# A two-layer graph block on one core: layer-one gates from row sums on VectorE, basis products in fours, and the layer norm's powers between the root weight's lower parts

## The chip, the cores and the metric

One core of a Trainium2 chip runs the whole program. The metric is device time in microseconds (us) for one execution. Five engines work side by side, each through its own queue of instructions: TensorE (PE in the profile, its weight loads PEld), VectorE (DVE), ScalarE (ACT), GpSimd (POOL) and SyncE (SP), which here issues the large loads. They hand work to each other with semaphores. The time that counts is the median of several executions; the profile shows one more, with its own time.

## The reference

625 nodes with 512 features, 20,625 edges of two types. First a graph convolution with batch norm, exact GELU and two residual sums, then a layer norm; its result is `x1`. On `x1` run two gated relational layers, and their sum with `x1` is normalised again:

```python
def rgcn_gate_layer(x, row, col, edge_type, basis, att, gate_w, root, bias):
    w = jnp.einsum('rb,bio->rio', att, basis)        # 30 bases of 512x512 -> 2 weights
    x_j = x[col]
    for r in range(NUM_RELATIONS):
        gate = jax.nn.sigmoid(x_j @ gate_w[r, :, 0])
        msgs.append(gate[:, None] * x_j @ w[r])
    msg = jnp.where((edge_type == 0)[:, None], msgs[0], msgs[1])
    agg = jax.ops.segment_sum(msg, row, num_segments=x.shape[0])
    return agg + x @ root + bias
...
h = relu(rgcn_gate_layer(x1, ..., basis1, ...)); out = rgcn_gate_layer(h, ..., basis2, ...)
```

A gate depends only on the node and the relation, so the kernel computes 625 x 2 gates and 625 x 2 products `Z` per layer and multiplies with count matrices of the edges afterwards.

## The kernel before

Nodes go in 5 chunks of 125 rows (`NC`), features in 4 blocks of 128 (`KC`). Matrix products of layers one and two run in single precision from two parts, an upper part rounded to fp32r and a lower part with the rest: `mm3` issues upper x upper, upper x lower and lower x upper (L542 to L544).

**The basis.** 64 parts of 1 MB (`basis_part`, L561) are contracted with the attention weights on TensorE: parts 0 to 31 for layer one, 32 to 63 for layer two. They go through a ring of 4 slots, `basis_ring`. SyncE issues the load of part n when part n - 4 has been used. `basis_upto(n)` places parts in TensorE's stream between other work, up to part n. 4 parts make one PSUM tile of `psW` (two tiles, used in turn), 8 parts one of 8 pairs of weight blocks. ScalarE empties the first tile (`w_first`), VectorE merges the second (`w_merge`), ScalarE makes the upper part (`w_high`) and VectorE the lower part (`w_low`).

**From the convolution to `x1`.** The convolved rows pass GELU on ScalarE, feature block by feature block, and are turned back on TensorE (L733). VectorE adds the residual (`x_sum`) and takes each chunk's mean and variance. GpSimd raises the variance to the power -0.5 (L518) and makes the bias (L519). ScalarE normalises (L962, `xs`), TensorE turns each chunk (`x1_turned`, L749), ScalarE and VectorE make the upper and lower parts in `hlT` (`x1_hi` L954, `x1_lo` L1281). The root weight is split by ScalarE (`root_hi`, L950) and GpSimd (`root1_low`, L511). GpSimd's stream puts three of the four lower parts ahead of the first power.

**Layer one.** 8 root products (2 halves of the nodes x 4 feature blocks) follow, with chunks 3 and 4 turned between them. Then `gates_and_z`: gate products of both halves (L779, 16 records), the first `Z`, the sums of their pairs (L799, 10 records), then the other nine `Z` of 12 matmuls each; TensorE waits for all of the layer's lower weight parts first. ScalarE copies the gate rows, takes the sigmoid and scales `Z` into `zg` (L998, L1328). Then 8 products `h` with the count matrices (L816), whose results become the next `hlT` (L1354, L1013, L1358).

**Layer two** is `gates_and_z(1)` again, then 5 chunks of `out` (root products and L836), the last layer norm and the stores. Four PSUM tiles of `psM` pass through a fixed list of uses; TensorE takes a tile when the use four places earlier has been emptied.

The order on every engine is written out by hand.

## Time and profile before

| | |
|---|---|
| median of 3 runs | 302.01 us (300.69 to 302.09) |
| the profiled execution | 302.61 us, its span 300.8 us |
| TensorE busy | 272.3 us, 91% of the span |
| VectorE / ScalarE / GpSimd busy | 158.6 / 84.4 / 48.0 us |
| mean granted TensorE clock | 0.983 of full |
| HBM read | 72.05 MB |

The span is the stretch between the first and the last recorded event of one execution; the remaining 1.8 us lie around it. Busy time says how long an engine worked, not whether the end of the program waited for it; the chain of waits says that. In timelines a row is: start, duration, engine, line, operation, output and inputs, shapes, number of instructions merged into the row, and in brackets the idle time before it with what ended it. The ends of matmuls are modelled, so the distance between two starts is the better measure.

### The profile page before, as it was taken

How to read it: one execution, taken by the hardware profiler on the slowest of the kernel's cores; microseconds unless marked ns; L12 is line 12 of the kernel's file. 1: busy time of each engine (PE TensorE's matmuls, PEld its weight loads, DVE VectorE, ACT ScalarE, POOL GpSimd, SP SyncE). 2: the span in 40 equal slices, each digit the busy share in tenths (PEclk: the TensorE clock that was granted, in tenths of full speed). 3: DMA queues.
4: the chain of work that ended last, by engine and by line, in shares of the span. 5: the costliest groups of instructions: out<-in, count | busy, mean ns of one | idle time of the engine just before them, and what ended most of it. 6: DMA issues, size and time to landing. Idle time of an engine off the chain costs nothing.

```text
span 300.8 us, 4592 instructions
## 1 busy us (share of the span) xinstructions
PE 272.3 (91%) x1687; PEld 182.4 (61%) x1687; DVE 158.6 (53%) x340; ACT 84.4 (28%) x143; POOL 48.0 (16%) x90
## 2 busy tenths in 40 slices
PE   0899889999799975999999999999989999999991
PEld 0784334335477742647666465677777787778770
DVE  6788878888738868726301412434242234234443
ACT  3351021003437586261531140114113242000000
POOL 5531000000681019000000000000009100011111
PEclk9999999999979999799999999999999999999997
DMA  6999999999899998999949788775004200001112
GB/s 170 222 418 385 403 403 405 407 380 349 300 287 340 367 386 331 392 377 391 382 168 419 279 358 340 278 264 237 2 0 105 72 1 0 0 2 34 34 34 68
DMA packets 12803, 73.64 MB, mean 245 GB/s; under 512 B 2000, under 2 KB 2243, under 8 KB 4588
## 3 DMA queue, kind: packets, MB, share of 16 engines
q1 hardware_dynamic: 11330, 70.82, 62.4%
q0 software_dynamic: 1104, 2.36, 3.1%
q8 instruction: 13, 0.21, 0.3%
q10 hardware_dynamic: 346, 0.17, 0.2%
q14 instruction: 10, 0.08, 0.1%
HBM read 72.05 MB, written 1.28 MB: 244 GB/s over the span
## 4 chain that ended last, share of the span: by engine, by line
PE 65%; DVE 14%; issue 6%; DMA 5%; ACT 4%; POOL 3%; DVEq 2%; SPq 0%; POOLq 0%; ACTq 0%
PE psW L561 12%; PE psM L542 9%; PE psM L543 8%; PE psM L544 8%; PE psM L816 8%; PE psM L836 6%; PE psM L692 3%; DVE B L1130 3%; DMA xs<-in_x_dram 3%; DMA basis_ring<-in_L_gnn_basis_dram 3%; PE psE L649 2%; POOL root_lo L511 2%; DVE w_full L1107 1%; PE psM L602 1%; DVEq L1120 1%
## 5 line engine op out<-in xcount | busy, mean ns | idle before, releaser
L561 PE MATMUL psW<-basis_ring,S 128*32 128x512 f32 x512 | 63.0, 608 | 2.4 <-DMA basis_ring<-in_L_gnn_basis_dram 2.0
L1328 DVE SCALAR_TENSOR_TENSOR zg<-psM,gate,zg 125x512 fp32r<-125x512 f32 x20 | 15.0, 750 | 57.0 <-ACT zg L998 57.0
L542 PE MATMUL psM<-w,hlT 128*125 128x512 f32 x80 | 32.4, 406 | 0.1
L561 PEld LDWEIGHTS psW<-basis_ring,S 128*32 128x32 f32 x512 | 13.3, 110 | 30.4 <-issue 21.1
L544 PE MATMUL psM<-w,hlT 128*125 128x512 f32 x80 | 31.6, 395 | 0.0
L543 PE MATMUL psM<-w,hlT 128*125 128x512 f32 x80 | 31.6, 395 | 0.0
L998 ACT ACTIVATE zg<-psM,gate 125x512 fp32r<-125x512 f32 x20 | 13.8, 689 | 46.3 <-PE psM L544 45.9
L649 PEld LDWEIGHTS psE<-oh_key,oh_src 128*125 128x125 f16 x162 | 14.0, 143 | 19.3 <-issue 15.6
L816 PEld LDWEIGHTS psM<-BB,zg 125*128 125x128 f32 x160 | 23.1, 188 | 3.4 <-issue 2.5
L816 PE MATMUL psM<-BB,zg 125*128 125x320 f32 (+1 forms) x160 | 24.1, 309 | 0.0
L836 PE MATMUL psM<-zg,BB 125*125 125x512 f32 x100 | 24.0, 394 | 0.0
L526 POOL DMA_DIRECT2D root_raw<-in_L_gnn_root_dram x16 | 7.9, 502 | 97.0 <-DVE hlT L1358 97.0
L1130 DVE TENSOR_TENSOR B<-B,psE 125x160 f32 x54 | 17.4, 323 | 8.5 <-issue 3.4
L836 PEld LDWEIGHTS psM<-zg,BB 125*125 125x125 f32 x100 | 18.6, 186 | 4.7
L616 PE MATMUL psM<-w0T,xT 128*125 128x512 f32 x40 | 20.3, 609 | 0.0
L542 PEld LDWEIGHTS psM<-w,hlT 128*125 128x125 f32 x80 | 14.8, 185 | 9.0 <-issue 2.5
L649 PE MATMUL psE<-oh_key,oh_src 128*125 128x160 f16 x162 | 17.2, 245 | 3.4 <-DVE B L1130 3.1
L1137 DVE TENSOR_TENSOR oh_key<-iota_f,key_pairs 128x960 f16<-128x960 f16 x27 | 18.1, 670 | 0.2
L544 PEld LDWEIGHTS psM<-w,hlT 128*125 128x125 f32 x80 | 14.8, 185 | 3.8
L543 PEld LDWEIGHTS psM<-w,hlT 128*125 128x125 f32 x80 | 14.8, 185 | 3.4
L692 PE MATMUL psM<-AT,z 125*128 125x320 f32 (+1 forms) x80 | 15.1, 340 | 1.6 <-DVE z L1223 1.6
L692 PEld LDWEIGHTS psM<-AT,z 125*128 125x128 f32 x80 | 13.0, 209 | 4.5 <-issue 3.5
(153 smaller groups left out, 385.0 us busy)
## 6 DMA issues: line engine op xcount, KB each, us to landing
basis_ring<-in_L_gnn_basis_dram SPq DMA_DIRECT2D x64, 1024.0 KB, 7.4
root_raw<-in_L_gnn_root_dram POOLq DMA_DIRECT2D x32, 64.0 KB, 2.9
xs<-in_x_dram SPq DMA_DIRECT2D x1, 1120.0 KB
out_dram<-xs SPq DMA_DIRECT2D x5, 224.0 KB
w_raw<-in_L_gnn_W_dram SPq DMA_DIRECT2D x4, 256.0 KB, 9.1
bias_b<-in_L_gnn_bias_dram POOLq DMA_DIRECT2D x1, 250.0 KB, 3.9
xs<-in_x_dram SPq DMA_DIRECT2D x1, 130.0 KB
out_dram<-xs SPq DMA_DIRECT2D x5, 26.0 KB
```

The source lines that it names most:

```text
L542: nc.tensor.matmul(o, l_hi, r_hi, start=start, stop=False)
L543: nc.tensor.matmul(o, l_hi, r_lo, start=False, stop=False)
L544: last[0] = nc.tensor.matmul(o, l_lo, r_hi, start=False, stop=stop)
L561: m = nc.tensor.matmul(psW[32 * j:32 * j + 32, cc % 2, :], S[:, cc % 2, cc // CH, q].rearrange("p k r -> p (k r)"), ring[:, n % RING, j, : ...
L616: last[0] = nc.tensor.matmul(bank(("xw", c))[0:PC, :], xT[:, k, n], w0T[:, k], start=(k == 0), stop=(k == KC - 1))
L649: nc.tensor.matmul(psE[0:PC, g % 2, at:at + KEYS], oh_src[:, g % 3, j * P:j * P + PC], oh_key[:, t % OH, :], start=(j % SG == 0), stop=(j ...
L692: last[0] = nc.tensor.matmul(bank(("agg0", f, h))[:, 0:n], z[:, i, s, f * P:(f + 1) * P], AT[:, s, a:a + n], start=(s == 0 and i == 0), st ...
L816: last[0] = nc.tensor.matmul(bank(("h", f, h))[:, 0:n], zg[:, i, d, r, f * P:(f + 1) * P], BB[:, at:at + n], start=(d + r + i == 0), stop= ...
L836: last[0] = nc.tensor.matmul(bank(("out", c))[0:PC, :], BB[:, at:at + PC], zg[:, i, d, r, :], start=False, stop=(d == NC - 1 and r + i == 2))
L1130: v.tensor_tensor(to, to, psE[0:PC, g % 2, h * KEYS:(h + 1) * KEYS] .rearrange("p (c t w) -> p c t w", c=NC, t=R), ALU.add).then_inc(win_a ...
L1137: return v.tensor_tensor(out, pair.unsqueeze(1).broadcast_to(shape), pairs[:, first:first + n].unsqueeze(2).broadcast_to(shape), ALU.is_equal)
L1328: link(v.scalar_tensor_tensor(out=zg[:, 1, c, r, :], in0=bank(("Z", L, c, r))[0:PC, :], scalar=gate[:, L, c, r:r + 1], in1=zg[:, 0, c, r, ...
```

## The change

- VectorE computes layer one's gates: GpSimd loads each gate vector of layer one into all 125 partitions (`gate_raw`, two DMAs ahead of the root weight's sixteen), ScalarE reorders them (`gate_q`, two copies before the third GELU), and VectorE takes ten row sums of `xs` times gate (`gates_dotted`), eight of them ahead of chunk 3's lower part. ScalarE's sigmoid reads these sums. TensorE has no gate work in layer one.
- In layer two each half's gate rows come just before the first `Z` that needs them, and the pair sums come in two groups.
- A `Z` waits for each lower weight part where it uses it.
- `basis_upto` is called with numbers that place four parts at a time from part 36 on.
- `w_merge(7)`, `w_high(7)` and `w_low(7)` stand earlier among the `h` products' results.
- GpSimd alternates: one lower part of the root weight, the power and bias of a chunk.

```diff
+            for r in range(R):
+                pool.dma_start(gate_raw[0:PC, r, :], gate1[r:r + 1, :, 0].broadcast_to([PC, D])).then_inc(gate1_in, 16)
...
-            for k in range(KC - 1):
-                root1_low(k)
             for c in range(NC):
+                if c < EARLY - 1:
+                    root1_low(c)
                 pool.wait_ge(var_ready, KC + 1 + c)
                 link(nc.gpsimd.tensor_tensor(lrs[:, c:c + 1], lrs[:, c:c + 1], mhalf[0:PC, 0:1], ALU.pow))
...
                 if c == EARLY - 1:
-                    root1_low(KC - 1)
+                    for k in range(c, KC):
+                        root1_low(k)
...
-                    basis_upto((35, 37, 39, 39, 41, 41, 43, 43)[KC * h + f])
+                    basis_upto((35, 39, 39, 39, 39, 43, 43, 43)[KC * h + f])
...
-                pe.wait_ge(w_lo, R * KC * (L + 1))
...
+                            pe.wait_ge(w_lo, R * (KC * L + k) + r + 1)
...
-                            basis_upto((45, 47, 47, 49, 51, 51, 53, 55, 55, 57)[R * c + r])
+                            basis_upto((43, 47, 47, 51, 51, 51, 55, 55, 55, 59)[R * c + r])
...
-                    basis_upto((57, 59, 59, 61, 61, 63, 63, 63)[KC * h + f])
-            gates_and_z(1)
+                    basis_upto((59, 59, 63, 63, 63, 63, 63, 63)[KC * h + f])
+            z_products(1)
...
+                if f == KC - 1:
+                    act.wait_ge(gate1_in, 16 * R)
+                    for r in range(R):
+                        nc.scalar.activation(in_q(gate_q[0:PC, r]), natural(gate_raw[0:PC, r]), ACT.Copy) \
+                            .then_inc(gate_q_ready, 1)
...
+                if L == 0:
+                    act.wait_ge(gate_dots, R * NC)
+                    link(nc.scalar.activation(gate[:, 0], gate_dot[:], ACT.Sigmoid))
...
-            w_high(7)
-            gates_and_z(1)
+                    if i == 5:
+                        w_high(7)
...
+            def gates_dotted(c):
+                dve.wait_ge(x1_ready, c + 1)
+                for r in range(R):
+                    link(v.scalar_tensor_tensor(out=gate_raw[0:PC, r], in0=xs[:, c, :], scalar=1.0, in1=gate_q[0:PC, r],
+                                                op0=ALU.mult, op1=ALU.mult, accum_out=gate_dot[:, c, r:r + 1]))
+                    dve.sem_inc(gate_dots, 1)
...
+            dve.wait_ge(gate_q_ready, R)
+            for c in range(NC - 1):
+                gates_dotted(c)
             x1_lo(3)
             w_low(2)
             x1_lo(4)
+            gates_dotted(NC - 1)
...
+                    if i == 4:
+                        w_merge(7)
                     if i == 6:
-                        w_merge(7)
-            w_low(7)
+                        w_low(7)
```

GpSimd, from the root weight's lower parts (`root_lo`) to chunk 3's power (`lrs`) and bias (`lnm`), before:

```order
L511 TENSOR_TENSOR root_lo<-root_raw,root_hi 128x512 x3
L518 TENSOR_TENSOR lrs<-lrs,mhalf 125x1
L519 TENSOR_TENSOR lnm<-lnm,lrs 125x1
L518 TENSOR_TENSOR lrs<-lrs,mhalf 125x1
L519 TENSOR_TENSOR lnm<-lnm,lrs 125x1
L518 TENSOR_TENSOR lrs<-lrs,mhalf 125x1
L519 TENSOR_TENSOR lnm<-lnm,lrs 125x1
L511 TENSOR_TENSOR root_lo<-root_raw,root_hi 128x512
```

And the same place now:

```order
L519 TENSOR_TENSOR root_lo<-root_raw,root_hi 128x512
L526 TENSOR_TENSOR lrs<-lrs,mhalf 125x1
L527 TENSOR_TENSOR lnm<-lnm,lrs 125x1
L519 TENSOR_TENSOR root_lo<-root_raw,root_hi 128x512
L526 TENSOR_TENSOR lrs<-lrs,mhalf 125x1
L527 TENSOR_TENSOR lnm<-lnm,lrs 125x1
L526 TENSOR_TENSOR lrs<-lrs,mhalf 125x1
L527 TENSOR_TENSOR lnm<-lnm,lrs 125x1
L519 TENSOR_TENSOR root_lo<-root_raw,root_hi 128x512 x2
```

The first power stands behind one lower part instead of three; the first three chunks' powers are past two lower parts, and two lower parts come behind them.

VectorE, from chunk 4's statistics of `x_sum` to the gate vectors' parts for layer two (`gw_hl`), before:

```order
L1289 BN_STATS lst<-x_sum 125x6
L1295 BN_AGGR lag<-lst 125x2
L1296 TENSOR_SCALAR lnm<-lag 125x1
L1265 TENSOR_SCALAR lrs<-lag 125x1
L1281 TENSOR_TENSOR hlT<-psM,hlT 128x4x125
L1116 TENSOR_TENSOR w<-w_full,w 128x512 x2
L1281 TENSOR_TENSOR hlT<-psM,hlT 128x4x125
L1316 CAST gw_hl<-vecT 128x8x2
```

Now:

```order
L1325 BN_STATS lst<-x_sum 125x6
L1331 BN_AGGR lag<-lst 125x2
L1332 TENSOR_SCALAR lnm<-lag 125x1
L1301 TENSOR_SCALAR lrs<-lag 125x1
L1339 SCALAR_TENSOR_TENSOR gate_raw,gate_dot<-xs,gate_q 125x512 x8
L1317 TENSOR_TENSOR hlT<-psM,hlT 128x4x125
L1152 TENSOR_TENSOR w<-w_full,w 128x512 x2
L1317 TENSOR_TENSOR hlT<-psM,hlT 128x4x125
L1339 SCALAR_TENSOR_TENSOR gate_raw,gate_dot<-xs,gate_q 125x512 x2
L1364 CAST gw_hl<-vecT 128x8x2
```

Eight row sums stand ahead of chunk 3's lower part (`hlT`), two behind chunk 4's.

TensorE, the last basis parts of layer two and the start of layer two's products, before (`BB,zg` are the `h` products, `hlT,gw_hl` the gate rows, `w,hlT` the first `Z`):

```order
L816 MATMUL psM<-BB,zg 128x320 x40
L561 MATMUL psW<-basis_ring,S 32x512 x8
L816 MATMUL psM<-BB,zg 128x306 x40
L561 MATMUL psW<-basis_ring,S 32x512 x8
L816 MATMUL psM<-BB,zg 128x306 x40
L779 MATMUL psM<-hlT,gw_hl 4x320 x8
L779 MATMUL psM<-hlT,gw_hl 4x306 x8
L542 MATMUL psM<-w,hlT 125x512
```

Now:

```order
L830 MATMUL psM<-BB,zg 128x320 x60
L570 MATMUL psW<-basis_ring,S 32x512 x16
L830 MATMUL psM<-BB,zg 128x320 x20
L830 MATMUL psM<-BB,zg 128x306 x80
L786 MATMUL psM<-hlT,gw_hl 4x320 x8
L551 MATMUL psM<-w,hlT 125x512
```

Three pairs of parts among the `h` products have become one four, and only the first half's gate rows stand ahead of the first `Z`. The rows count matmuls as written; the profile has two records for each of `psW`, the gate rows and the pair sums.

## Rows read from the trace of the kernel before

**Rows 1.** The page: the chain that ended last, by engine.
```profile
PE 65%; DVE 14%; issue 6%; DMA 5%; ACT 4%; POOL 3%; DVEq 2%; SPq 0%; POOLq 0%; ACTq 0%
```
**Rows 2.** Timeline before layer two: TensorE alone, start and duration first.
```profile
222.84 1.32 PE L779 MATMUL psM<-hlT,gw_hl 128*4 128x320 f32 x8
225.88 1.28 PE L779 MATMUL psM<-hlT,gw_hl 128*4 128x306 f32 x8 [1.71 <-DVE hlT L1358]
227.21 0.50 PE L542 MATMUL psM<-w,hlT 128*125 128x512 f32 x1
```
**Rows 3.** Timeline before layer one's `Z`: gate rows, first `Z`, pair sums.
```profile
147.87 2.44 PE L779 MATMUL psM<-hlT,gw_hl 128*4 128x320 f32 x16
150.15 0.39 PE L542 MATMUL psM<-w,hlT 128*125 128x512 f32 x1
153.02 1.25 PE L799 MATMUL psM<-pair_sum,gate_rows 4*125 4x2 f32 x10
```
**Rows 4.** Timeline of TensorE, one pair of basis parts among the root products.
```profile
138.53 0.30 PE L544 MATMUL psM<-hlT,root_lo 128*128 128x306 f32 x1
138.76 1.92 PE L561 MATMUL psW<-basis_ring,S 128*32 128x512 f32 x16
140.62 0.41 PE L542 MATMUL psM<-hlT,root_hi 128*128 128x306 f32 x1
144.21 1.07 PE L561 MATMUL psW<-basis_ring,S 128*32 128x512 f32 x8
```
**Rows 5.** Timeline from the fourth GELU to the normalised chunks, several engines.
```profile
108.76 0.91 ACT L944 ACTIVATE hf<-hf,bn 128x625 f32<-128x625 f32 x1 [0.78 <-DVE bn L1234]
110.71 4.03 ACT L950 ACTIVATE root_hi<-root_raw 128x512 fp32r<-128x512 f32 x4
111.85 4.59 POOL L511 TENSOR_TENSOR root_lo<-root_raw,root_hi 128x512 fp32r<-128x512 f32 x3 [3.79 <-ACT root_hi L950]
116.36 0.58 POOL L518 TENSOR_TENSOR lrs<-lrs,mhalf 125x1 f32<-125x1 f32 x1
117.31 1.53 ACT L962 ACTIVATE xs<-x_sum,lnm,lrs 125x512 f32<-125x512 f32 x2 [2.57 <-POOL lnm L519]
```
**Rows 6.** Timeline of the basis parts 30 to 35 on TensorE.
```profile
111.95 2.78 PE L561 MATMUL psW<-basis_ring,S 128*32 128x512 f32 x24
115.92 1.07 PE L561 MATMUL psW<-basis_ring,S 128*32 128x512 f32 x8 [1.19 <-DMA basis_ring<-in_L_gnn_basis_dram]
121.23 2.99 PE L561 MATMUL psW<-basis_ring,S 128*32 128x512 f32 x16
122.69 0.45 PEld L561 LDWEIGHTS psW<-basis_ring,S 128*32 128x32 f32 x8 [1.26 <-DMA basis_ring<-in_L_gnn_basis_dram]
```
**Rows 7.** Stretches: busy us by engine, granted clock, DMA share, GB/s.
```profile
113.10:114.20 1.10, 1.10 (x16) 0.28 (x8) 1.06 (x5) 1.10 (x2) 1.10 (x2) 1.00 0.41 82
114.20:152.20 38.00, 34.41 (x237) 21.84 (x230) 19.67 (x45) 17.37 (x30) 7.29 (x13) 0.96 0.98 384
152.20:156.10 3.90, 3.90 (x31) 2.00 (x29) 0.60 (x1) 0.89 (x3) 0.00 (x0) 1.00 0.07 29
156.10:166.80 10.70, 10.70 (x59) 7.03 (x60) 1.65 (x3) 1.42 (x3) 0.00 (x0) 1.00 0.99 390
```
**Rows 8.** The ring's tile: its loads from issue to landing.
```profile
DMA to landing us min/median/max: 4.7/7.4/18.5
```
**Rows 9.** VectorE: chunk 3's lower part, and a linked operation with two inputs.
```profile
133.49 0.68 DVE L1281 TENSOR_TENSOR hlT<-psM,hlT 128x500 fp32r<-128x500 f32 x1 [5.29 <-ACT hlT L954]
138.71 0.74 DVE L1102 SCALAR_TENSOR_TENSOR w_half<-psW,mask_h,w_half 128x512 f32<-128x512 f32 x1
110.13 1.02 DVE L1274 SCALAR_TENSOR_TENSOR x_sum<-xs,psM 125x512 f32<-125x512 f32 x1 [1.41 <-PE psM L733]
```
**Rows 10.** Stretches ahead of the spell of low clock and in it; the page's clock.
```profile
116.00:120.50 4.50, 2.58 (x18) 1.21 (x19) 3.33 (x8) 3.17 (x5) 4.00 (x8) 0.95 1.01 415
120.50:123.80 3.30, 3.30 (x20) 0.96 (x18) 2.23 (x4) 0.72 (x2) 0.00 (x0) 0.56 1.00 420
PEclk9999999999979999799999999999999999999997
```

More of the change, by code:

```diff
@@ L182, in gnn_block @@
         gate = sb("gate", [PC, 2, NC, R], F32)
+        gate_dot = sb("gate_dot", [PC, NC, R], F32)
         psM = ctx.enter_context(nc.psum_tensor("psM", [P, 4, 512], F32))
@@ L285, in gnn_block @@
                     use(("x1T", LATE[h, f]), "dve")
+        ROWS_AT = {(0, 0): 0, (1, 0): 1}
+        GATE_AT = {(0, 0): 0, (1, 0): 1}
+        GATED = (range(0, HALF[0][1] // PC), range(HALF[0][1] // PC, NC))
         for L in range(2):
-            for h in range(2):
-                use(("gate_rows", L, h), "act")
             for c in range(NC):
                 for r in range(R):
+                    if L == 1 and (c, r) in ROWS_AT:
+                        use(("gate_rows", ROWS_AT[c, r]), "act")
                     use(("Z", L, c, r), "dve")
-                    if (c, r) == (0, 0):
-                        use(("gate", L), "act")
+                    if L == 1 and (c, r) in GATE_AT:
+                        use(("gate", GATE_AT[c, r]), "act")
             if L == 0:
@@ L766, in _, with gate_rows_of, gates_turned, z_products @@
                         x1_turned(LATE[h, f])
[L767 to L784 removed]
+                    basis_upto((35, 39, 39, 39, 39, 43, 43, 43)[KC * h + f])
+            def gate_rows_of(h):
+                a, n = HALF[h]
+                pe.wait_ge(gw_ready, 1)
+                pe.wait_ge(t_ready, NC + (h + 1) * KC)
+                wait_free(pe, ("gate_rows", h))
+                for k in range(KC):
+                    for i in range(2):
+                        last[0] = nc.tensor.matmul(bank(("gate_rows", h))[0:2 * R, 0:n],
+                                                   gw_hl[:, 1, k].rearrange("p i r -> p (i r)"),
+                                                   hlT[:, i, k, a:a + n], start=(k + i == 0),
+                                                   stop=(k == KC - 1 and i == 1))
+                done()
+            def gates_turned(h):
+                pe.wait_ge(gate_rows_ready, h + 1)
+                wait_free(pe, ("gate", h))
+                for i, d in enumerate(GATED[h]):
+                    last[0] = nc.tensor.matmul(bank(("gate", h))[0:PC, R * i:R * i + R],
+                                               gate_rows[:, d * PC:(d + 1) * PC], pair_sum[:], start=True, stop=True)
+                done()
+            def z_products(L):
                 for c in range(NC):
@@ L793, in gates_and_z @@
                         done()
-                        if (c, r) == (0, 0):
-                            pe.wait_ge(gate_rows_ready, 2 * (L + 1))
-                            wait_free(pe, ("gate", L))
-                            for d in range(NC):
-                                last[0] = nc.tensor.matmul(bank(("gate", L))[0:PC, R * d:R * d + R],
-                                                           gate_rows[:, d * PC:(d + 1) * PC], pair_sum[:],
-                                                           start=True, stop=True)
-                            done()
+                        if L == 1 and (c, r) in GATE_AT:
+                            gates_turned(GATE_AT[c, r])
                         if L == 0:
-                            basis_upto((45, 47, 47, 49, 51, 51, 53, 55, 55, 57)[R * c + r])
-            gates_and_z(0)
+                            basis_upto((43, 47, 47, 51, 51, 51, 55, 55, 55, 59)[R * c + r])
+            z_products(0)
             for h, (a, n) in enumerate(HALF):
@@ L999, in gates_and_z @@
                                              scale=gate[:, L, c, r:r + 1]).then_inc(zg_hi, 1)
+                        if L == 1 and (c, r) == (1, 0):
+                            gates_of(1)
                     if L == 0 and c == 2:
@@ L1322, in z_parts @@
             def z_parts(L):
-                dve.wait_ge(gate_ready, L + 1)
                 for c in range(NC):
+                    dve.wait_ge(gate_ready, L + 1 + (L == 1 and c in GATED[1]))
                     for r in range(R):
```

57 lines of the change are left out of this document (27 added, 30 removed).

## The prediction

> **What bounds the kernel now.** I read the chain of waits first: TensorE carries 65% of what ended last, and no other engine more than 14% [rows 1]. So work taken off TensorE counts in full, unless TensorE then waits for something else. The timelines of its gaps come next. Before layer two it stands still for 1.71 us until the last block of `hlT` is ready [rows 2]. Before layer one it waits twice for basis parts, part 33 until 115.92 and part 35 until 122.69 [rows 6]. Last come the stretches by DMA share: from 114.2 to 152.2 the DMA engines are 98% busy, with no reserve, and only later do they pause, at a share of 0.07 from 152.2 to 156.1 [rows 7]. The reader should keep two regimes apart: until about 150 the ring of basis parts sets the pace together with TensorE, afterwards TensorE alone does.
>
> **What TensorE loses.** Layer one's gate rows: from 147.87 to the first `Z` at 150.15 are 2.3 us, less one normal step, 2.1 us [rows 3]. Layer one's pair sums: 1.25 us, 1.2 after the same step [rows 3].
>
> The fours: one more part within a group costs 2.78 - 1.92 = 0.86 us [rows 4, 6]. A pair costs more than 2 x 0.86 = 1.72: from the last root matmul's start ahead of it at 138.53 to the first one's behind it at 140.62 are 2.09 us, less one normal step of 0.14, so 1.95 [rows 4]; the two root products behind it take 3.59 us up to 144.21, some 0.05 of that a slow first step. That makes a seam of about 0.28. Fourteen pairs (36 to 63) become seven fours: 7 x 0.28 = 2.0 us. A four takes 3.7.
>
> Layer two's seam: the wait of 1.71 us goes, since the first half's gate rows and the first two chunks' `Z` need nothing of the second half, and block 7's weight parts, now made two `h` products earlier, no longer end at 227.2. What is late next is the sigmoid of two chunks; it has a whole `Z` of 2.9 us [rows 3] ahead of it, and four PSUM tiles. Two more seams take back what is left of the gap up to 227.21. I take 1.7.
>
> Together 7.0 us, if nothing starves.
>
> **The front, with the GpSimd move.** The power of chunk 0 stands behind 4.59 us of lower parts, 1.53 each, and ScalarE idles 2.57 us for it [rows 5]. Behind one part it would be 3.06 us earlier. But ScalarE gets two reordering copies ahead of the third GELU. They have no row; the nearest is `root_hi` with the same reordering, 4.03 / 4 = 1.0 us each [rows 5]. The fourth GELU, at 108.76, had 0.78 us of idle time before it [rows 5], which hides that much. Bounds: 0 if the copies ran in idle time altogether, 2.0 if nothing hid them; I take 2.0 - 0.8 = 1.2 us. Everything behind moves by that: `root_hi` 110.7 to 111.9, its end 114.7 to 115.9. ScalarE can normalise chunk 0 only then, at about 116.0 instead of 117.31. A power with its bias takes about 0.8 (from 116.36 to shortly before 117.31). Chunk 2's ended at 116.36 + 2.4 = 118.8 before; now it comes behind two lower parts and two powers, 113.05 + 3.06 + 2.4 = 118.5. The last lower part ends 1.4 us later, near 121.7, and the root products cannot start before 35 in any case. So the two edits nearly cancel there.
>
> Part 35 decides. It landed at 122.69, and SyncE could issue it only when part 31 had been used, 1.7 us into the group at 111.95 [rows 6]. That group stands behind GELU and moves with it, up to 1.2 us. The DMA engines had nothing but stragglers at that moment (share 0.41 in 113.1 to 114.2 [rows 7]), so the load may land up to 1.2 later, or at the same time if the straggler sets it. I take +0.35 us for the root products' start, bounds -0.5 and +1.2.
>
> The two loads of gate vectors add 0.5 MB, 1.3 us of the rate of 390 GB/s, at 82 us, and two issues ahead of sixteen on GpSimd's queue; the root weight is not read before 110.7, so nothing waits. Bounds 0 and 1.3, taken 0.
>
> **VectorE's row sums.** No row shows this form. The nearest linked operation takes 0.74 us, a reordered one 1.02 [rows 9]. VectorE was idle for 5.29 us ahead of chunk 3's lower part at 133.49, so it was free from 128.2 [rows 9]. With 0.8 each, eight sums end at 128.2 + 6.4 = 134.6, 1.1 us later than that start. Chunk 4's part then ends at about 138.4, and the fifth root product, which needs it, comes at about 138.8. That costs nothing; with 1.02 each the product would wait 1.5 us.
>
> **What starves.** The ring has four slots. A load alone takes 4.7 us to land [rows 8]; four loads in a row take 10.7 us of the DMA engines [rows 7], 2.67 each. So the fourth lands 1.0 + 4.7 + 3 x 2.67 = 13.7 us after a four begins, and is wanted 2.75 us into the next. Two fours must be 11 us apart. At the first one (36 to 39) parts 38 and 39 are issued only when 34 and 35 have been used, before at about 122 and at 124.2 [rows 6]. Behind 35 at 122.69 four loads of 2.67 give 133.4; with the front's delay 134.1. TensorE wants it at 124.2 + 0.35 + two products (3.6) + chunk 3's turn (an estimate of 0.6: four small transposes) + three parts (2.6) = 131.4. It waits 2.7 us; bounds 1.5 and 4. Between the second and third four lie more than 11 us, fine. The fourth (48 to 51) follows after two `Z` only, 3.7 + 5.6 = 9.3 us: it waits 1.4; bounds 0.6 and 3. The others are 12 us apart or more: 0.
>
> **Sum.** 302.61 - 7.0 + 0.35 + 2.7 + 1.4 = 300.06. I round the waits down by 0.1, to 299.9, since chunk 2's power comes 0.3 us earlier. The profiled execution lies 0.6 above the median of the runs, so I forecast 299.3 us as a median, 0.9% less. About 0.5% (1.5 us) is what can be told from no change.
>
> **Rivals.**
>
> A: the ring does not starve, because the stragglers and not the issues set the landing. For it: in all pairs behind 150 TensorE never waited for a part. Against it: a DMA share of 0.98 up to 152. Then 302.0 - 7.0 + 0.35 = 295.4.
>
> B, slower: the new waits cost TensorE its clock. Before, 4.5 us with 2.58 busy were followed by 3.3 us at a granted clock of 0.56, near the lower of its two levels, 1.2 GHz [rows 10]; work of 3.3 x 0.44 = 1.45 us was lost. If each of three places (in front of the root products longer than now, at the first four, at the fourth) brought one such spell, 4.35 us would be added: 299.3 + 4.35 = 303.7. It decides from the second spell on: two give 302.2. Against it: the wait of 1.71 us before layer two [rows 2] brought no spell, the clock's digits there are all 9 [rows 10]. The Trainium skill says on this, in "TensorE: Matmul & The Clock Gate", section "The HAM clock gate", that the throttled state is the default and activity releases it, so a starved TensorE is slowed again; by that rule the longer wait at the first four would be followed by slow products, by the row of 1.71 us it would not.
>
> C: the change does not do what it says at the front and VectorE is late. Row sums at 1.02 to 1.1 us hold the fifth root product back by 1.5 to 2, and part 35 lands the full 1.2 late: 299.3 + 1.5 + 0.85 = 301.6, no measurable change.
>
> **How the numbers follow.** Forecast 0.48, its own range 297.8 to 300.8; A 0.20; B 0.17; C 0.15. Eight in ten: from A's 295.2 up to 302.6, where half of B is left out. Faster by over 0.5% (below 300.5): 0.46 of the forecast, 0.20 of A, 0.04 of C, 0.70. Same: 0.02 + 0.10 of C + 0.04 of B = 0.16. Slower: 0.14.
>
> **What would show it.** Right: the root products start near 124.5; TensorE waits for `basis_ring` by 2 to 3 us in the first four and by about 1.4 in the one after the fourth `Z`; layer one's first `Z` starts within half a microsecond of 150.15; the last `h` product ends near 222.5; the first `Z` of layer two follows 1.3 us behind. ScalarE normalises chunk 0 near 116.0, after `root_hi`, not after a power. Wrong: no waits for the ring at the fours (A), a granted clock near 0.5 behind one (B), or a fifth root product that VectorE releases (C). If `xs` for chunk 0 started near 114 the reordering copies cost nothing, and the front would gain too.

## The result, and the profile after

| | before | after |
|---|---|---|
| median | 302.05 us (4 runs, 300.69 to 303.11) | 298.75 us (4 runs, 296.8 to 301.16) |
| the profiled execution, its span | 302.61, 300.8 us | 299.43, 297.6 us |
| TensorE busy | 272.3 us | 267.4 us |
| VectorE busy | 158.6 us | 165.3 us |

The ratio is 0.9899 with an interval of 0.9861 to 0.9936, so the kernel became 1.0% faster; 299.3 was forecast. Beside three other kernels on another chip the same kernel had 298.63 us and 0.9896 [0.9852, 0.994]. The total is right, but it is a sum of terms of which one, the start of the root products, was far off, and others made up for it. The chain that ended last, by engine:

```profile
PE 63%; DMA 19%; DVE 8%; issue 4%; ACT 2%; DVEq 2%; POOL 1%; SPq 0%; POOLq 0%; ACTq 0%
```

TensorE kept its share, and DMA went from 5% [rows 1] to 19%. Waits for the ring replace the work taken off TensorE. The timeline of TensorE after the change, at the waits and at the start of each stage:

```profile
98.40 1.06 PE L570 MATMUL psW<-basis_ring,S 128*32 128x512 f32 x8
101.92 1.06 PE L570 MATMUL psW<-basis_ring,S 128*32 128x512 f32 x8 [2.46 <-DMA basis_ring<-in_L_gnn_basis_dram]
113.96 5.34 PE L570 MATMUL psW<-basis_ring,S 128*32 128x512 f32 x32
122.34 1.06 PE L570 MATMUL psW<-basis_ring,S 128*32 128x512 f32 x8 [0.44 <-DMA basis_ring<-in_L_gnn_basis_dram]
124.83 1.07 PE L570 MATMUL psW<-basis_ring,S 128*32 128x512 f32 x8 [1.43 <-DMA basis_ring<-in_L_gnn_basis_dram]
125.83 0.41 PE L551 MATMUL psM<-hlT,root_hi 128*128 128x320 f32 x1
132.28 1.06 PE L570 MATMUL psW<-basis_ring,S 128*32 128x512 f32 x8 [0.34 <-DMA basis_ring<-in_L_gnn_basis_dram]
143.09 0.30 PE L553 MATMUL psM<-hlT,root_lo 128*128 128x306 f32 x1
143.33 3.64 PE L570 MATMUL psW<-basis_ring,S 128*32 128x512 f32 x32
146.90 0.41 PE L551 MATMUL psM<-hlT,root_hi 128*128 128x306 f32 x1
147.15 0.30 PE L552 MATMUL psM<-hlT,root_hi 128*128 128x306 f32 x1
150.39 0.39 PE L551 MATMUL psM<-w,hlT 128*125 128x512 f32 x1
169.50 1.06 PE L570 MATMUL psW<-basis_ring,S 128*32 128x512 f32 x8 [1.31 <-DMA basis_ring<-in_L_gnn_basis_dram]
221.75 1.33 PE L786 MATMUL psM<-hlT,gw_hl 128*4 128x320 f32 x8
222.92 0.40 PE L551 MATMUL psM<-w,hlT 128*125 128x512 f32 x1
225.80 0.59 PE L797 MATMUL psM<-pair_sum,gate_rows 4*125 4x2 f32 x4
229.20 1.25 PE L786 MATMUL psM<-hlT,gw_hl 128*4 128x306 f32 x8
```

Part 27 now waits at 101.92, where before nothing waited (its group stands at 99.84 there, one row of 1.92 us). Part 35 starts at 124.83 instead of 122.69 [rows 6]. The root products start 1.7 us later than before (125.83 and 124.15), and layer one's first `Z` still comes at 150.39, against 150.15 [rows 3]. Layer two's first `Z` comes 1.17 us behind the first gate rows, where it was 4.37 us [rows 2]. ScalarE at the front, after:

```profile
107.02 2.02 ACT L957 ACTIVATE gate_q<-gate_raw 125x512 f32<-125x512 f32 x2
108.95 0.89 ACT L963 ACTIVATE hf<-hf,bn 128x625 f32<-128x625 f32 x1
110.79 0.89 ACT L963 ACTIVATE hf<-hf,bn 128x625 f32<-128x625 f32 x1
112.73 3.96 ACT L969 ACTIVATE root_hi<-root_raw 128x512 fp32r<-128x512 f32 x4
116.57 0.82 ACT L981 ACTIVATE xs<-x_sum,lnm,lrs 125x512 f32<-125x512 f32 x1
```

The copies take 1.01 us each. The fourth GELU comes at 110.79 against 108.76 [rows 5], and chunk 0 is normalised at 116.57 right behind `root_hi`; its power and bias end at about the same time, at 116.42.

### The profile page after: what moved, and what is told of

It reads as the page before. It is cut to its first block, busy times and chain, and to the rows that moved or that the text cites. A ratio compares the mean times of both kernels' runs of the same rounds, so it can differ in the third digit from the quotient of the medians.

```text
span 297.6 us, 4596 instructions
## 1 busy us (share of the span) xinstructions
PE 267.4 (90%) x1661; PEld 179.6 (60%) x1661; DVE 165.3 (56%) x360; ACT 85.8 (29%) x144; POOL 49.6 (17%) x92
## 4 chain that ended last, share of the span: by engine, by line
PE 63%; DMA 19%; DVE 8%; issue 4%; ACT 2%; DVEq 2%; POOL 1%; SPq 0%; POOLq 0%; ACTq 0%
DMA basis_ring<-in_L_gnn_basis_dram 16%; PE psW L570 13%; PE psM L551 8%; PE psM L553 8%; PE psM L552 8%; PE psM L830 8%; PE psM L850 6%; PE psE L658 3%; DMA xs<-in_x_dram 3%; DVE B L1166 2%; PE psM L701 2%; PE psM L625 2%; PE psM L611 1%; DVEq L1156 1%; DVE oh_key L1173 1%
## 5 line engine op out<-in xcount | busy, mean ns | idle before, releaser
L570 PE MATMUL psW<-basis_ring,S 128*32 128x512 f32 x512 | 64.2, 624 | 8.2 <-DMA basis_ring<-in_L_gnn_basis_dram 7.9
L570 PEld LDWEIGHTS psW<-basis_ring,S 128*32 128x32 f32 x512 | 14.0, 112 | 41.2 <-issue 22.7
L1423 DVE TENSOR_TENSOR res<-res,psM 125x512 f32<-125x512 f32 x5 | 3.4, 688 | 21.2 <-PE psM L850 21.2
L1173 DVE TENSOR_TENSOR oh_src<-iota_f,place_pairs 128x756 f16<-128x756 f16 x27 | 14.9, 552 | 0.4 <-DVE w_full L1143 0.2
```

Source lines behind the costliest of these rows:

```text
L570: m = nc.tensor.matmul(psW[32 * j:32 * j + 32, cc % 2, :], S[:, cc % 2, cc // CH, q].rearrange("p k r -> p (k r)"), ring[:, n % RING, j, : ...
L1173: return v.tensor_tensor(out, pair.unsqueeze(1).broadcast_to(shape), pairs[:, first:first + n].unsqueeze(2).broadcast_to(shape), ALU.is_equal)
```

## The experiments

All edits are on the kernel after, except the two said to be on the kernel before. "Part 27" gives the wait in front of that part and "root" the start of the root products, both in the profiled execution, in us; "-" means that this profile isn't used.

| | median, runs | ratio to before [95%] | part 27 | root |
|---|---|---|---|---|
| after | 298.75, 4 | 0.9899 [0.9861, 0.9936] | 2.46 | 125.83 |
| after, on a second chip | 298.63, 6 | 0.9896 [0.9852, 0.994] | 2.04 | 126.24 |
| GpSimd's order of before | 299.77, 12 | 0.9945 [0.991, 0.9979] | 2.17 | 127.89 |
| basis parts in pairs | 298.62, 6 | 0.9898 [0.9866, 0.9931] | 2.75 | 125.86 |
| copies late | 297.95, 6 | 0.9884 [0.9856, 0.9911] | 0 | 123.01 |
| copies late, second chip | 297.04, 6 | 0.9858 [0.9808, 0.9909] | 0 | 122.68 |
| copies late, pairs | 298.54, 6 | 0.9879 [0.9839, 0.9918] | 2.63 | 124.71 |
| no gate loads | 298.59, 6 | 0.9886 [0.9853, 0.9919] | 0 | 125.10 |
| gate loads twice | 300.62, 12 | 0.9934 [0.9902, 0.9966] | - | - |
| block 7 late | 299.96, 12 | 0.9923 [0.9899, 0.9948] | 2.80 | 126.75 |
| pairs and fours mixed | 300.32, 9 | 0.992 [0.9886, 0.9955] | 0 | 125.02 |
| before with GpSimd's new order | 301.4, 12 | 0.996 [0.9935, 0.9985] | 0 | 122.45 |
| before with fours | 302.14, 12 | 0.9999 [0.9967, 1.0031] | 0 | 124.30 |

**GpSimd's order of before.** The edit on the kernel after:

```diff
+            for k in range(KC - 1):
+                root1_low(k)
             for c in range(NC):
-                if c < EARLY - 1:
-                    root1_low(c)
...
                 if c == EARLY - 1:
-                    for k in range(c, KC):
-                        root1_low(k)
+                    root1_low(KC - 1)
```

> The changed kernel with GpSimd's old order: three lower parts of the root weight ahead of the first power. Theory (basis parts set the start of the root products): chunk 0 is normalised about 2.7 us later (near 119.3 instead of 116.6), but part 35 still lands near 124.8, so the root products start at most 0.7 us later and the median is 298.7 to 299.5. Rival (the powers were on the path): the root products start 2 us or more later and the median rises to about 301.

The median rose by 1.0 us. In the profile the three lower parts (115.59, 4.57 us) stand ahead of the first power again and chunk 0 is normalised at 121.03; no part of the ring is waited for at 34 and 35, so the normalisation is the bound there. The root products come 2.06 us later than after, as the rival had it, though the median stays near the theory's range. The fairer profile beside it is the second one of the kernel after: it has the same spell of low clock behind part 27 and reaches part 30 at the same time (115.57, here 115.68), and its root products start at 126.24. Of the 1.65 us between the two, 0.1 stands there already, 1.1 is low clock over parts 34 and 35, and about 0.4 is the order itself:

```profile
124.95 3.01 PE L569 MATMUL psW<-basis_ring,S 128*32 128x512 f32 x16
```

From here to the first root product are 2.94 us; the same stretch at full clock, with no wait, takes 1.85 (late copies with pairs, 122.86 to 124.71). The kernel before has 2.92 (121.23 to 124.15 [rows 6]) and the kernel before with fours 2.96. So the clock was low over parts 34 and 35 in all three profiles with GpSimd's old order, where TensorE stood 2.4 to 2.6 us, in one wait or two, ahead of chunk 0's turn, and in none of the other ten compared. That the longer stand brings the low clock is argued from this, not shown.

**The kernel before with GpSimd's new order alone.** The same lines, the other way round:

```diff
-            for k in range(KC - 1):
-                root1_low(k)
...
+                if c < EARLY - 1:
+                    root1_low(c)
...
-                    root1_low(KC - 1)
+                    for k in range(c, KC):
+                        root1_low(k)
```

> The kernel before with GpSimd's new order alone. Theory (part 35 sets the start of the root products where GELU is not delayed): chunk 0 is normalised 2 us earlier, near 115, but part 35 still lands near 122.7 and the root products start at most 0.5 us earlier than 124.15; median 301.3 to 301.7. Rival (the powers were the path, as the changed kernel with the old order let one think, 1.1 us slower): the root products start 1.1 us or more earlier, median 300.6 or less.

0.4% faster (0.15 to 0.65). Chunk 0 is normalised at 114.49 instead of 117.31. TensorE:

```profile
119.26 1.07 PE L562 MATMUL psW<-basis_ring,S 128*32 128x512 f32 x8
121.46 1.06 PE L562 MATMUL psW<-basis_ring,S 128*32 128x512 f32 x8 [1.13 <-DMA basis_ring<-in_L_gnn_basis_dram]
122.45 0.41 PE L543 MATMUL psM<-hlT,root_hi 128*128 128x320 f32 x1
```

The root products start 1.70 us earlier than before, where the theory allowed 0.5 at most: the rival is right on the start, though the median lies in the theory's range. Part 34 comes 1.97 us earlier (121.23 before), and only now does TensorE wait for part 35. So in the kernel before the powers, and not part 35, held the root products back. Part of the 1.70 us is lost again at chunk 4's turn, which waits 1.01 us instead of 0.48.

**Basis parts in pairs**, the three lists of `basis_upto` as before:

```diff
-                    basis_upto((35, 39, 39, 39, 39, 43, 43, 43)[KC * h + f])
+                    basis_upto((35, 37, 39, 39, 41, 41, 43, 43)[KC * h + f])
...
-                            basis_upto((43, 47, 47, 51, 51, 51, 55, 55, 55, 59)[R * c + r])
+                            basis_upto((45, 47, 47, 49, 51, 51, 53, 55, 55, 57)[R * c + r])
...
-                    basis_upto((59, 59, 63, 63, 63, 63, 63, 63)[KC * h + f])
+                    basis_upto((57, 59, 59, 61, 61, 63, 63, 63)[KC * h + f])
```

> The changed kernel with basis parts placed in pairs as before (35, 37, 39, ... 63). Theory: seven more seams of 0.28 us cost 2.0 us, the waits of the fours for the ring (1.9 us at parts 38 and 39, 1.3 us at part 51) go, so the time is 1.2 us lower, 297.5. Rival (fours gain what their seams say): 2 us higher, 300.8.

No difference: 298.62 against 298.75, so neither expectation came true. The waits for the ring behind the root products' start go (3.03 us in the kernel after), and others come, of 0.4 and 0.75 us. TensorE in pairs, the rows that wait between 126 and 222 us:

```profile
134.31 0.41 PE L758 MATMUL psM<-ident,xs 125*128 125x125 f32 x2 [0.40 <-ACT r1T L993]
139.49 0.41 PE L551 MATMUL psM<-hlT,root_hi 128*128 128x306 f32 x1 [0.75 <-DVEq L1321]
```

The first row is chunk 4's turn, which waits for ScalarE. The kernel before has the same wait (132.70, 0.48 us), and the prediction had overlooked it. The second is the fifth root product: behind pairs it comes early enough to wait for VectorE, which is late by the row sums. In the kernel after the wait for the ring covers both.

**The kernel before with fours alone**, these three lists the other way round:

> The kernel before with nothing but the basis parts in fours. By the prediction's terms alone: -2.0 for seven seams, +2.7 and +1.4 for the waits at parts 36 to 39 and 48 to 51, so about +2.1, less what is absorbed later: 302.5 to 304. If the fours are worth what they cost, as they were on the changed kernel, it stays within 0.5 us of before, near 301.8. In the profile the waits should stand at the first and at the fourth group of four only.

Ratio 0.9999. TensorE there:

```profile
132.77 1.07 PE L561 MATMUL psW<-basis_ring,S 128*32 128x512 f32 x8 [1.37 <-DMA basis_ring<-in_L_gnn_basis_dram]
144.92 1.06 PE L561 MATMUL psW<-basis_ring,S 128*32 128x512 f32 x8 [0.77 <-DMA basis_ring<-in_L_gnn_basis_dram]
172.31 1.06 PE L561 MATMUL psW<-basis_ring,S 128*32 128x512 f32 x8 [1.39 <-DMA basis_ring<-in_L_gnn_basis_dram]
```

The waits stand at the first and the fourth four, as expected, and also at the second (144.92). Taken from start to start, the three fours last 4.3 us longer than undisturbed ones (their first parts are at 128.49, 141.37 and 168.14, and an undisturbed last part comes 2.58 us behind its first). Chunk 4's turn saves 0.7, the root products start 0.15 later, and the span grew by 1.6 (302.4 against 300.8), so the seven seams gave 4.3 + 0.15 - 0.7 - 1.6 = 2.1 us, 0.3 each. In the medians nothing is left of the 1.6. Both kernels say the same: fours exchange seams for waits.

**Pairs and fours mixed**, so that no four comes early:

```diff
-                    basis_upto((35, 39, 39, 39, 39, 43, 43, 43)[KC * h + f])
+                    basis_upto((35, 37, 39, 39, 39, 43, 43, 43)[KC * h + f])
...
-                            basis_upto((43, 47, 47, 51, 51, 51, 55, 55, 55, 59)[R * c + r])
+                            basis_upto((43, 47, 47, 47, 51, 51, 51, 55, 55, 57)[R * c + r])
```

> The changed kernel with basis parts placed for the ring: pairs for 36 to 39 and 56 to 59, fours elsewhere, and 48 to 51 one Z later, 52 to 55 one Z later. Theory (fours gain only where the ring is full): of the waits of 1.9 us at the first four about 0.4 are left, that of 1.3 us at part 51 goes, two more seams cost 0.6 us: 2.2 us lower, 296.5. Rival (the waits are only shifted to the next part, since the DMA rate sets them): same median as the changed kernel, 298.7.

It isn't better: the waits at parts 38 and 39 are gone, and the next four waits instead. TensorE, and one stretch (busy us by engine, granted clock, DMA share, GB/s):

```profile
144.23 1.06 PE L570 MATMUL psW<-basis_ring,S 128*32 128x512 f32 x8 [0.80 <-DMA basis_ring<-in_L_gnn_basis_dram]
146.71 1.93 PE L570 MATMUL psW<-basis_ring,S 128*32 128x512 f32 x8 [1.42 <-DMA basis_ring<-in_L_gnn_basis_dram]
```
```profile
146.00:151.00 5.00, 4.29 (x20) 2.62 (x21) 0.00 (x0) 1.27 (x2) 0.00 (x0) 0.66 1.02 423
```

The waits are 2.2 us here and 0.5 at 208.42, against 1.7 and 1.3 in the kernel after: about as much in either form, so they go with the rate of the loads more than with the grouping. And right behind this wait the clock is at 0.66 of full over 5 us, which loses another 5 x 0.34 = 1.7. That is rival B's mechanism.

**The copies late.** ScalarE copies the gate vectors only behind chunk 2's upper part (in the loop over the chunks, once `x1_hi(2)` is issued):

```diff
-                if f == KC - 1:
-                    act.wait_ge(gate1_in, 16 * R)
-                    for r in range(R):
-                        nc.scalar.activation(in_q(gate_q[0:PC, r]), ...
...
+                    act.wait_ge(gate1_in, 16 * R)
+                    for r in range(R):
+                        nc.scalar.activation(in_q(gate_q[0:PC, r]), ...
```

> The changed kernel with ScalarE's two reordering copies of the gate vectors moved from ahead of the third GELU into its idle time behind chunk 2's upper part. Theory (the copies delay GELU, with it the group of parts 30 to 33 and so the issue of part 35): the group starts 1.5 to 2 us earlier, part 35 lands 1 to 2 us earlier, the root products start about 1.5 us earlier, median 297.2. Rival (the DMA engines' rate sets part 35): it lands when it did, and the median stays at 298.7.

And once more beside the kernel after on one chip. The edit is the same two copies; the text below describes them wrongly (three copies, ahead of `root_hi`):

> The changed kernel with ScalarE's three copies of the gate rows behind the second chunk's normalisation instead of ahead of the root weight's upper parts. If the copies delay the front on the way to the root products (theory: they push x and the root weight's upper parts 2 us back, and about half of it reaches TensorE), the time is 0.7 to 1.0 us below the unaltered changed kernel beside it, near 298.0. If the front is set by the ring's transfers (rival: the third group of basis parts waits for its transfer whatever ScalarE does), it stays within 0.3 us of it.

Both are below the kernel after, by 0.8 and 1.6 us in the medians. With all runs of the two kernels, each divided by the median of before in its own comparison, the means have a ratio of 0.996 [0.992, 1.000] (12 and 10 runs): about 0.4%, at the edge of what can be told from nothing. Of the second, ScalarE and TensorE:

```profile
108.92 0.91 ACT L958 ACTIVATE hf<-hf,bn 128x625 f32<-128x625 f32 x1 [0.78 <-DVE bn L1269]
110.87 3.97 ACT L964 ACTIVATE root_hi<-root_raw 128x512 fp32r<-128x512 f32 x4
114.72 0.83 ACT L976 ACTIVATE xs<-x_sum,lnm,lrs 125x512 f32<-125x512 f32 x1
120.11 2.04 ACT L984 ACTIVATE gate_q<-gate_raw 125x512 f32<-125x512 f32 x2
```
```profile
100.00 1.93 PE L570 MATMUL psW<-basis_ring,S 128*32 128x512 f32 x16
112.11 3.64 PE L570 MATMUL psW<-basis_ring,S 128*32 128x512 f32 x32
121.68 1.06 PE L570 MATMUL psW<-basis_ring,S 128*32 128x512 f32 x8 [1.10 <-DMA basis_ring<-in_L_gnn_basis_dram]
122.68 0.42 PE L551 MATMUL psM<-hlT,root_hi 128*128 128x320 f32 x1
131.59 1.07 PE L570 MATMUL psW<-basis_ring,S 128*32 128x512 f32 x8 [1.39 <-DMA basis_ring<-in_L_gnn_basis_dram]
137.33 0.41 PE L551 MATMUL psM<-hlT,root_hi 128*128 128x306 f32 x1 [0.48 <-DVEq L1320]
```

GELU, `root_hi` and the group of parts 30 to 33 are back at their old places (112.11, before 111.95 [rows 6]), chunk 0 is normalised at 114.72, the copies lie in idle time, and the root products start 3.15 us earlier than after. That is more than the copies: in this execution part 27 isn't waited for, and no low clock lies on parts 30 to 33 (four parts in 3.64 us, after in 5.34). The sum is worked out below. The four parts behind keep their distance to part 35 (131.59 - 121.68 = 9.91; after 134.72 - 124.83 = 9.89), so the waits there don't grow with an earlier front.

**The copies late, with pairs**, the two edits above together.

> The same kernel with late copies, and the basis parts in pairs as in the kernel before. If fours only exchange seams (seven of about 0.28 us) for waits on the ring (about 1.8 to 2.7 us), pairs are the same to 0.5 us, 297.5 to 298.5. If the earlier front made the fours' waits longer (TensorE reaches parts 36 to 39 earlier than their transfers), pairs win here by about 1 us, 297.0.

298.54, 0.9879 [0.9839, 0.9918]: not told apart from the fours beside it. Chunk 4's turn waits 2.03 us for ScalarE, which is itself held up by chunk 4's power; the fifth root product doesn't wait. The clock is low behind this wait:

```profile
135.00:139.00 4.00, 4.00 (x21) 0.98 (x20) 3.32 (x9) 1.43 (x4) 0.00 (x0) 0.57 0.93 320
```

In this profile the next bound among the root products is the path of chunk 4, not the ring.

**Without the loads of the gate vectors.** The copies read rows of `x` instead, so layer one's gates come from other numbers; all work but the two loads is unchanged.

```diff
-            for r in range(R):
-                pool.dma_start(gate_raw[0:PC, r, :], gate1[r:r + 1, :, 0].broadcast_to([PC, D])).then_inc(gate1_in, 16)
...
-                        nc.scalar.activation(in_q(gate_q[0:PC, r]), natural(gate_raw[0:PC, r]), ACT.Copy) \
+                        nc.scalar.activation(in_q(gate_q[0:PC, r]), natural(xs[:, r, :]), ACT.Copy) \
```

> The changed kernel without the two loads of gate vectors; the reordering copies read rows of x instead, so layer one's gates are of other numbers. Theory (0.5 MB more on full DMA engines delay the basis parts): TensorE's wait of 2.46 us for part 27 near 99.5 falls to about 1.2 us or less and all behind it comes 1.2 us earlier, median 297.5. Rival (that wait is there only because TensorE came 1.4 us earlier by a luckier clock): the end of the wait stays at 101.9 and the median at 298.7.

298.59, no difference. In its profile part 27 isn't waited for and the group of parts 30 to 33 starts at 112.99. Everything up to the copies lies as in the kernel with late copies (parts 28 and 29 at 105.63 and 105.60), so the copies alone cost TensorE 112.99 - 112.11 - 0.03 = 0.85 us. The kernel after says the same: its group starts 7.33 us behind part 28, with late copies 6.51.

**The loads twice**, once more into the copies' own tile:

```diff
+            for r in range(R):
+                pool.dma_start(gate_q[0:PC, r, :], gate1[r:r + 1, :, 0].broadcast_to([PC, D])).then_inc(gate1_in, 16)
...
-                    act.wait_ge(gate1_in, 16 * R)
+                    act.wait_ge(gate1_in, 16 * 2 * R)
```

> The changed kernel with the two gate loads done twice, 1 MB instead of 0.5, the second time into the space that the copies fill later. Theory (their bytes come out of the ring's rate): the wait for part 27 ends 1.3 us later than at 101.9, and the median rises by about 1.0, to 299.8. Rival (they are hidden; the run without them was no faster): same wait, same median, 298.7.

300.62, 0.9934 [0.9902, 0.9966]: 1.9 above after in the medians, but with intervals that meet, so a cost of another 0.5 MB isn't told from nothing. The theory's sign isn't there: in the profiled execution, one of the two longest of its twelve, the wait for part 27 ends at 102.00 (after: 101.92) and not 1.3 us later.

**Block 7 late**, its three steps where they were before:

```diff
-                    if i == 5:
-                        w_high(7)
...
+            w_high(7)
...
-                    if i == 4:
-                        w_merge(7)
...
-                        w_low(7)
+                        w_merge(7)
+            w_low(7)
```

> The changed kernel with block 7's merge, upper and lower parts back at their old places behind the h products. Theory (the split of the gate rows and the wait per weight part removed the gap before layer two, the earlier block 7 hardly counts): the first Z waits at most 0.5 us for its last quarter, median 298.7 to 299.2. Rival (the weights were what the gap waited for): 1.3 us or more, 300.0.

299.96. The first `Z` of layer two comes 1.16 us behind the gate rows, as in the kernel after, and within it TensorE waits once:

```profile
226.84 0.49 PE L551 MATMUL psM<-w,hlT 128*125 128x512 f32 x1 [0.34 <-DVE w L1151]
```

So the earlier block 7 is worth 0.34 us, and the split gate rows (with the wait for each lower part where it is used) made the rest, which no run tests by itself. That the medians differ by 1.2 isn't explained by this row; 0.9 of it stands already at the root products' start, ahead of the edit.

**The kernel after once more**, unaltered:

> The changed kernel unaltered, beside three others on one chip, so that small differences can be read. The earlier comparison gave a ratio of 0.9899 to the kernel before, so about 298.9 us is expected here. If the position of the low-clock spells is what moves a run (each costs about 1.7 us of full clock), single runs should spread over some 3 to 4 us, and the profiled run may show the root products' start anywhere from 124 to 128.

298.63; single runs from 297.86 to 301.16.

## Why the prediction was right, step by step

All entries are distances from start to start. A wait taken in this way is a little longer than its bracket, which goes by modelled ends.

| step | predicted | in the profile |
|---|---|---|
| root products' start | +0.35 | +1.7 |
| gate rows, layer one | -2.1 | -2.3 |
| pair sums, layer one | -1.2 | -1.2 |
| seven seams | -2.0 | -2.2 |
| chunk 4's turn | not seen | -0.7 |
| wait in the first four | +2.7 | +2.1 |
| wait in the fourth four | +1.4 | +1.5 |
| layer two's seam | -1.7 | -2.1 |
| sum | -2.55 | -3.2 (span: -3.2) |

The first line is 1.3 us worse than predicted and the others together 2.0 better. That the total came out as forecast is therefore in part luck, all the more since the first line depends on where spells of low clock fell in the two profiled executions. In the chances, A's time of 295.4 became 295.2 in the range of eight in ten, and by the chances given that range holds some nine in ten; neither changes the forecast.

**TensorE's work, right.** Between the last root matmul (150.25) and the first `Z` (150.39) stands nothing, no pair sums follow, and no product waits for the gates. The gate rows cost 150.15 - 147.87 = 2.28 us, since the first `Z` takes the place at which they began; the prediction took one step too many off. A seam includes the slow first step behind a group, so the second root matmul behind it is the one to measure to. Before, behind the pair at 138.76 [rows 4]:

```profile
140.86 0.31 PE L543 MATMUL psM<-hlT,root_hi 128*128 128x306 f32 x1
```

A pair takes 140.86 - 138.53 - 2 x 0.14 = 2.05 us, a four 147.15 - 143.09 - 2 x 0.14 = 3.78. So a seam is 2 x 2.05 - 3.78 = 0.32; I had 0.28, and seven give 2.2. From the first `Z` to the first `h` product the profile has +1.06 us; four fours for seven pairs (15.1 - 14.35), 1.5 at the wait for the ring and -1.2 for the pair sums make the same.

**The front, the step that failed.** "I take +0.35 us for the root products' start, bounds -0.5 and +1.2." It was +1.68, outside the bounds. Two things in this step were wrong.

First, "part 35 decides" holds after the change, but not before it. The row at 122.69 [rows 6] is one of weight loads, which run ahead of the matmuls; TensorE itself has no wait there, and with its clock low over parts 34 and 35 it comes to the first root product 2.92 us behind part 34, in the same time as two other executions with low clock there (2.94 and 2.96). What TensorE waited for last was chunk 2's normalisation, and so the powers; the kernel before with GpSimd's new order bears it out. Before:

```profile
120.20 1.10 PE L749 MATMUL psM<-ident,xs 125*128 125x125 f32 x4 [0.66 <-ACT xs L962]
```

"So the two edits nearly cancel there" was therefore said of a place that did decide.

Second, the load of part 35 is issued when part 31 has been used, and what delays part 31 delays part 35. SyncE's issues of part 35, after and with late copies (second chip):

```profile
117.52 0.33 SPq L426 DMA_DIRECT2D basis_ring<-in_L_gnn_basis_dram  x1
```
```profile
114.10 0.33 SPq L426 DMA_DIRECT2D basis_ring<-in_L_gnn_basis_dram  x1
```

| profile | group of parts 30 to 33 | clock over it | issue of 35 | part 35 starts |
|---|---|---|---|---|
| before with GpSimd's new order | 111.87 | full | 113.86 | 121.46 |
| late copies, second chip | 112.11 | full | 114.10 | 121.68 |
| mixed | 112.83 | low | 116.38 | 124.03 |
| no gate loads | 112.99 | low | 116.60 | 124.11 |
| after | 113.96 | low | 117.52 | 124.83 |
| after, second chip | 115.57 | full | 117.55 | 125.24 |

Part 35 starts 7.3 to 7.7 us behind its issue in all six (7.1, 7.8 and 7.9 with pairs, block 7 late and late copies on the first chip), and the issue comes 2.0 us behind the group's start at full clock, but 3.5 to 3.6 at low clock. A spell of low clock on this group thus costs 1.6 us at part 35. The 3.15 us between the kernel after and late copies are then: 1.0 for the wait at part 27 (parts 28 and 29 at 106.63 and 105.60), 0.8 for the copies, 1.6 for the low clock on parts 30 and 31, less 0.3 since this load took 7.3 us and not 7.6. The kernel before lies 1.47 us behind late copies, 1.1 of it low clock on parts 34 and 35 and the remaining 0.4 the wait for the powers; 3.15 - 1.47 = 1.68.

So the copies were taken too dear (1.2, measured 0.8 to 0.85), and halving them was wrong too, since all of it reaches part 35. But 1.0 and 1.3 of the 3.15 us were no term of the sum: the wait at part 27, and a low clock where it delays the ring. In its second profile the kernel after has full clock on this group and a spell ahead of it, and starts its root products at 126.24.

Is the wait at part 27 due to the loads of the gate vectors, which I had taken at 0? In the thirteen profiled executions compared (all but that with doubled loads), it goes with the time at which TensorE reached parts 22 and 23:

| start of parts 22 and 23 | kernels | wait for part 27 |
|---|---|---|
| 85.50 to 86.01 | after (both), GpSimd's old order, pairs, late copies with pairs, block 7 late | 2.04 to 2.80, part 27 at 101.92 to 102.66 |
| 86.83 to 87.17 | before, both edits of before, late copies (both), no gate loads, mixed | none, group at 99.77 to 100.06 |

Late copies have the loads in either row, so the loads alone don't bring the wait. Whether it would come without them is not shown: all four profiles without loads lie in the second row. The early ones ran their slow clock over parts 20 and 21 at about 77 to 81 us, the late ones over the convolution at 82 to 87; two of either kind had two spells in a row. Stretches from 90 to 98 us of before, after and late copies:

```profile
90.00:98.00 8.00, 8.00 (x73) 6.47 (x72) 6.55 (x21) 5.82 (x9) 1.12 (x2) 1.00 0.97 346
90.00:98.00 8.00, 8.00 (x75) 6.47 (x73) 6.17 (x20) 6.31 (x10) 1.73 (x3) 1.00 1.04 290
90.00:98.00 8.00, 8.00 (x75) 6.47 (x74) 6.54 (x21) 5.73 (x10) 1.52 (x3) 1.00 1.02 354
```

With the DMA engines full in all three, the kernel after moves 290 GB/s and the others 346 and 354; over all thirteen it is 277 to 306 in the first row of the table and 312 to 354 in the second. GpSimd issues the root weight's sixteen loads just ahead of it, from 82.3 to 90.2 us after. Why the loads go slower when TensorE is 1.4 us ahead stays open. So does whether the kernel before ever runs that way: its three profiles, two of them with an edit, don't.

**The waits for the ring, right in kind.** The distance from part 35 to part 39 is 9.9 us where I had 4 x 2.67 = 10.7: a load in that row takes 2.47, not the 2.67 of the later stretch. This 0.8 is most of the difference between 2.7 and 2.1 (134.72 against 132.6, where part 39 would have come undisturbed). The fourth four lost 1.5, where 1.4 was worked out, and no other four waited. Rival A falls, and the "mixed" experiment shows why: parts come at a rate.

**VectorE's row sums, right.** One takes 0.69 us and its accumulator read 0.08, one every 0.85; after, chunk 4's turn and the fifth product stand behind a wait for the ring that covers them. In six other profiles the fifth root product waits for VectorE: 0.38 us in the second one of the kernel after, 0.19 and 0.48 with late copies, 0.55 mixed, 0.75 with pairs, 1.16 with GpSimd's old order. Rival C's second half is real, below its price of 1.5 to 2.

**Layer two's seam, right, for one of two reasons.** -3.2 up to the first `Z`, +1.1 behind it for the second gate rows: -2.1. Block 7 carries 0.3 of it; that the split rows carry the rest is what remains, not a run of its own.

**Rival B, partly true.** In the kernel after, 2.46 us of waiting at 101.92 were followed by full clock; in the same kernel on the second chip and with GpSimd's old order, waits of 2.04 and 2.17 at the same place were followed by low clock. The stretch behind part 27 there, first with GpSimd's old order, then after:

```profile
102.00:107.00 5.00, 4.90 (x28) 4.02 (x29) 1.94 (x5) 0.56 (x2) 0.00 (x0) 0.66 1.01 397
102.00:107.00 5.00, 5.00 (x42) 3.87 (x46) 2.42 (x7) 1.32 (x3) 0.00 (x0) 1.00 1.01 413
```

The clock is at 0.66 of full in the first, a mixture of its two levels of 1.2 and 2.4 GHz, and at full in the second. Each such spell loses about 1.7 us of full clock; up to the last `out` product the profiles here had one to four of them (before and after two each, late copies one). Where it falls matters too: on parts 30 to 33 it also puts part 35 off by 1.6 us, as worked out above. The Trainium skill's "TensorE: Matmul & The Clock Gate", section "What's actually happening", says that the throttled state is the default, that activity releases it, and that the point of the change varies. The runs here fit it: two of the six waits at part 27 in the table were followed by a slow spell, and four were not. So B's mechanism exists, as a property of a run more than of the kernel, and may be one reason why runs of one kernel lie 3 to 4 us apart. That it is the main reason wasn't shown.

## What to carry to other kernels

An operation put into the idle time of an engine costs what isn't idle directly behind it, and where that engine leads to the release of a ring slot, the whole rest appears at the landing of the load that waits for the slot, as does a spell of low clock there: place it where the engine waits anyway (here behind chunk 2's upper part: the lowest median of all kernels tried, 297.04 us beside 298.63). When a ring is fed at the rate at which it is emptied, other groupings only move the waits; what is saved at seams comes back as waiting. A weight load that the profile releases by a DMA isn't a wait of TensorE: look at the matmul row beside it before calling that load the bound. And two profiles of kernels that differ in little have to be compared group by group from well ahead of the change, since a difference that is there already isn't the edit's.

## What the runs showed of the hardware that I had not expected

- GpSimd's power takes 0.55 us, but 0.93 beside a row sum on VectorE, whose next row sum then starts 1.20 us behind it and not 0.85. After, chunk 4's power:

```profile
129.16 0.93 POOL L526 TENSOR_TENSOR lrs<-lrs,mhalf 125x1 f32<-125x1 f32 x1 [3.33 <-DVE lrs L1301]
```
```profile
129.00 0.68 DVE L1339 SCALAR_TENSOR_TENSOR gate_raw<-xs,gate_q 125x512 f32<-125x512 f32 x1
129.60 0.08 DVE L1339 DVE_READ_ACCUMULATOR gate_raw<-xs,gate_q 125x1 f32 x1
130.20 0.70 DVE L1339 SCALAR_TENSOR_TENSOR gate_raw<-xs,gate_q 125x512 f32<-125x512 f32 x1 [0.51 <-DVE gate_raw L1339]
```

  The Trainium skill's "SBUF — State Buffer", section "SBUF: two separate sides", says that a VectorE operation with two inputs in SBUF and a GpSimd operation that reads SBUF lock each other out for a whole instruction. These rows fit it: 0.93 - 0.55 = 0.38 us.
- The DMA engines moved 277 to 306 or 312 to 354 GB/s over the same 8 us at a share of 0.91 to 1.05, and the lower rates went with a TensorE that was 1.4 us ahead.
- A sum with an accumulator costs 0.85 us from start to start for 125 x 512, 0.08 of it the read.
